# A mixture-of-experts block on one core: 58 feed-forward units of one form in engine loops, five token groups, roots and sigmoid from exp and ln

## What is computed

```python
def _mlp(x, wfc, wproj):
    h = jnp.square(jax.nn.relu(x @ wfc))
    return h @ wproj
shared = _mlp(x, w_fc_sh, w_proj_sh)
logits = xf @ router_w.T
scores = jax.nn.sigmoid(logits)
_, idx = jax.lax.top_k(scores + balance_bias, 2)
tw = jnp.take_along_axis(scores, idx, axis=-1)
tw = tw / (tw.sum(-1, keepdims=True) + 1e-20)
combine = (jax.nn.one_hot(idx, E) * tw[..., None]).sum(1)
h = jnp.square(jax.nn.relu(jnp.einsum('nc,ech->neh', xf, w1)))
y = jnp.einsum('neh,ehc->nec', h, w2)
routed = jnp.einsum('nec,ne->nc', y, combine)
...
h = h + _L0_attn_ref(_layernorm(h), ...)
h = h + _L0_ffn_ref(_layernorm(h), ...)      # shared + routed
```

## Time and profile before

| | us |
|---|---|
| median of three runs | 1073.99 (1067.09 to 1076.02) |
| the profiled execution | 1071.89 |
| its span | 1069.8 |
| PE busy | 633.5 |
| DVE busy | 723.8 |
| ACT busy | 480.2 |
| POOL busy | 301.6 |

### The profile page before, as it was taken

The page is one execution under the profiler, slowest core; times in us unless marked ns, Lnnn a source line. Parts: engine busy times, 40 slices in busy tenths (PEclk is TensorE's granted clock), DMA queues, the critical chain, the costliest instruction groups (busy, mean ns, idle before and its releaser), DMA issues.

```text
span 1069.8 us, 20111 instructions
## 1 busy us (share of the span) xinstructions
PE 633.5 (59%) x6510; PEld 480.5 (45%) x6510; DVE 723.8 (68%) x1727; ACT 480.2 (45%) x826; POOL 301.6 (28%) x269
## 2 busy tenths in 40 slices
PE   3669899045750777058888884412221389959462
PEld 2669699034640444025455553311111267747341
DVE  3314454378995999789999999888342575527265
ACT  3112253023445454058888885444311158747330
POOL 2111000056861111013232221103363700141455
PEclk9989799566695555556555555555555689969685
DMA  7953462220000222022222224410111324537343
GB/s 184 243 140 101 117 147 85 79 64 1 0 1 27 68 83 62 14 43 33 45 39 45 39 39 99 190 52 33 42 60 44 118 75 136 163 105 202 87 121 115
DMA packets 150683, 89.35 MB, mean 84 GB/s; under 512 B 88376, under 2 KB 143232, under 8 KB 150496
## 3 DMA queue, kind: packets, MB, share of 16 engines
q1 hardware_dynamic: 142768, 68.94, 25.3%
q0 software_dynamic: 7856, 19.68, 6.3%
HBM read 45.62 MB, written 28.51 MB: 69 GB/s over the span
## 4 chain that ended last, share of the span: by engine, by line
PE 24%; SPq 20%; DVE 19%; issue 15%; another core or an unknown queue 9%; ACT 6%; DMA 4%; POOL 4%; DVEq 0%; POOLq 0%; ACTq 0%
PE ps L1641 19%; SPq L564 7%; ACT R L718 3%; DMA R<-h_rows 2%; DVE M L1224 2%; DVE M L1225 2%; SPq L536 2%; SPq L543 2%; SPq L542 2%; SPq L544 1%; POOL R L711 1%; PE ps L1715 1%; PE ps L1896 1%; SPq L484 1%
## 5 line engine op out<-in xcount | busy, mean ns | idle before, releaser
L1641 PE MATMUL ps<-R 128*128 128x256 f16 (+6 forms) x2024 | 310.6, 308 | 91.9 <-issue 42.5
L1641 PEld LDWEIGHTS ps<-R 128*128 128x128 f16 (+3 forms) x2024 | 220.8, 131 | 154.7 <-issue 113.8
L718 ACT ACTIVATE R<-ps 128x768 f16<-128x768 f16 (+5 forms) x217 | 139.7, 662 | 183.9 <-remote 74.6
L1641 PE MATMUL ps<-M 32*128 32x68 bf16 (+4 forms) x1192 | 101.7, 245 | 99.3 <-DMA M<-R 65.9
L1641 PEld LDWEIGHTS ps<-M 32*128 32x128 bf16 (+3 forms) x1192 | 65.7, 116 | 151.3 <-issue 61.2
L721 ACT ACTIVATE R<-R,sc 128x512 f16<-128x512 f32 (+11 forms) x107 | 83.8, 839 | 92.8 <-POOL R L669 41.1
L711 POOL DMA_INDIRECT R<-y_by_tile,M x68 | 65.5, 963 | 143.7 <-DMA y_by_tile<-R 106.2
L683 POOL TENSOR_TENSOR R<-R,M 128x884 f32<-128x884 f32 x32 | 53.2, 1662 | 148.2 <-ACT M L840 148.2
L702 POOL DMA_INDIRECT x_by_expert<-R,M x68 | 66.1, 973 | 88.3 <-DVEq L1517 68.5
L718 ACT ACTIVATE R<-R 128x512 f16<-128x512 f32 (+4 forms) x101 | 64.7, 642 | 57.7 <-POOL R L652 20.4
L1641 PE MATMUL ps<-M,R 128*68 128x192 f16 (+2 forms) x430 | 47.1, 259 | 52.3 <-DVE R L1410 21.9
(11 more groups left out here) (281 smaller groups left out, 1148.4 us busy)
## 6 DMA issues: line engine op xcount, KB each, us to landing
R<-x_by_expert SPq DMA_DIRECT2D x41, 192.0 KB
y_by_tile<-R SPq DMA_DIRECT2D x41, 192.0 KB
R<-in_x_dram SPq DMA_DIRECT2D x12, 576.0 KB, 11.5
M<-R SPq DMA_DIRECT2D x16, 260.0 KB, 2.3
M<-R SPq DMA_DIRECT2D x32, 130.0 KB, 2.0
R<-w_split SPq DMA_DIRECT2D x1, 4032.0 KB, 23.2
R<-h_rows SPq DMA_DIRECT2D x4, 816.0 KB
R<-h_rows SPq DMA_DIRECT2D x1, 3264.0 KB, 14.3
```

The source lines that it names most:

```text
L718: return act.activation(out_, in_, ACT.Copy)
L1641: return pe.matmul(o, a, b, start=start, stop=stop, skip_group_check=True)
```

## The change

The feed-forward part and the groups are written anew.

- `WINDOWS` has five groups of 1, 4, 4, 4 and 4 pairs, and `SHARED_FIRST` is 12.
- All 58 units have one form. The rows of the shared pairs are stored to `x_by_expert` too, behind the routed ones (`SHARED_ROW`). SP loads the rows of every unit by a row number from a table, into one of eight sets (`XR`); TensorE turns them (`turn_unit`); ScalarE copies every result to `yr` and SP stores it in `y_by_unit`. For a pair's shared part SP loads its stored result again (`load_shared`) and VectorE adds it at the start of `combine`; `add_shared` is gone. `LAG` is 2.
- TensorE, ScalarE, VectorE and SP run the units in engine loops, two units a turn on TensorE, four on ScalarE, two or eight on VectorE, eight on SP. TensorE's groups are a loop as well. Since the set and the expert aren't known when the loop is written, TensorE reads three numbers of a table `rows_i` in each unit: the set's place before the transposes, the weights' place before `up` and again before `down`.
- `rows_i` lies on one partition: `make_table` now has 40 columns and 6 scan steps, and two of its columns go over TensorE and PSUM to that partition; `unit_rows` writes the shared units' part early.
- The roots are Exp(0.5 Ln v), and the sigmoid is Exp on ScalarE followed by an addition and a reciprocal on VectorE in `choose`. Normalising moves from VectorE to ScalarE (`x2_high`). The weights of all tokens are worked out once behind the table (`weigh`) and no longer in each `choose`.
- The combining starts at unit 33, one pair for two units, and pairs 12 to 16 are combined after the last unit. `combined` starts at 4, so that POOL may gather four pairs before the first is combined.

The core of the diff:

```diff
-WINDOWS = [(0, 5), (5, 12), (12, 17)]
-SHARED_FIRST = 10
+WINDOWS = [(0, 1), (1, 5), (5, 9), (9, 13), (13, 17)]
+SHARED_FIRST = 12
...
-            def load_tile(t):
-                wait(sp, "tile_turned", t - 3)
-                at = sp.value_load(table[t:t + 1, 1:2], min_val=0, max_val=XROWS - TILE)
+            for i in range(PAIRN):
+                sp.wait_ge(sem("rows2"), i + 1)
+                at = SHARED_ROW + TILE * i
+                sp.dma_start(xg[at:at + TILE, :].rearrange("(a p) c -> p a c", p=P), rows2[:, 2 * i:2 * i + 2, :]).then_inc(sem(f"x_rows{i // SHARED_FIRST}"), 16)
+            def load_unit(u, slot_, turn_):
+                wait(sp, "unit_turned", u - XR + 1)
+                wait(sp, f"xr{slot_ % 2}", 16 * (turn_ * (XR // 2) + slot_ // 2))
+                at = sp.value_load(rows_i[0:1, 1, bass.ds(u, 1)], min_val=0, max_val=XROWS - TILE)
...
+            def load_shared(i, slot_, turn_):
+                sp.wait_ge(sem("combined"), i + 1)
...
             def roots(k):
-                act.activation(rs2[:, 1, t], rs2[:, 0, t], ACT.Sqrt).then_inc(sem("ln2_sqrt"), 1)
+                chain(act, "scalar_step", act.activation(rs2[:, 1, t], rs2[:, 0, t], ACT.Ln))
+                act.activation(rs2[:, 1, t], rs2[:, 1, t], ACT.Exp, scale=0.5).then_inc(sem("ln2_sqrt"), 1)
             def x2_high(i):
-                act.wait_ge(sem("xf"), i + 1)
+                act.wait_ge(sem("ln2_done"), window_of(i) + 1)
+                for j in range(2):
+                    n = 2 * i + j
+                    last = ident_(xf[:, i % 2, j, :], hf[:, n, :], scale=rs2[:, 2, n:n + 1], bias=rs2[:, 0, n:n + 1])
...
             def choose(w):
+                ch(ts(s, s, 1.0, None, ALU.add))
+                ch(dve.reciprocal(s, s))
...
-            for w in range(3):
-                turn_window(w)
-                rank(w)
+            with pe.Fori(0, NW - 1) as w:
+                for j in range(4):
+                    turn_rows(w * 4 + 1 + j, j)
+                    if j >= 1:
+                        route(w * 4 + j, j - 1)
+                route(w * 4 + 4, 3)
+                rank(w + 1, w * 8 + 2, 8)
...
-            def turn_tile(t):
+            def turn_unit(u, par, half):
+                pe.wait_ge(sem(f"xr{par}"), half * 16 + 16)
+                wait(pe, "unit_x", u - 1)
+                at = pe.value_load(rows_i[0:1, 2, bass.ds(u, 1)], min_val=0, max_val=(XR - 1) * 4 * C)
+                        last = pe.transpose(o[:, (2 * k + j) * P:(2 * k + j + 1) * P], xr_flat[:, bass.ds(at + 2 * C * j + c, P)], ident_f[:, :])
...
-            def load_expert(u):
-                if kind == "r":
-                    expert_at.append(pe.value_load(table[i:i + 1, 0:1], min_val=0, max_val=E * WB))
+            def up(u, par, half):
+                at = pe.value_load(rows_i[0:1, 0, bass.ds(u, 1)], min_val=0, max_val=E * WB)
...
+            def down(u, par, half):
+                at = pe.value_load(rows_i[0:1, 0, bass.ds(u, 1)], min_val=0, max_val=E * WB)
...
-            for u in range(UNITS + LAG):
-                if 0 <= t + 1 < ROUTED:
-                    turn_tile(t + 1)
-                if u < UNITS:
-                    load_expert(u)
-                    up(u)
-                if u >= LAG:
-                    down(u - LAG)
+            pipeline(pe, [(turn_unit, 0), (up, 1), (down, 1 + LAG)], UNITS)
```

More of the change, by code:

```diff
@@ L64, with pipeline @@
 C0 = 0.35815147
-def pipeline(eng, stages, groups):
+def pipeline(eng, stages, groups, ring=2):
     last = max(lag for _, lag in stages)
-    lead = last + 2 + (groups - last) % 2
+    lead = last + 2
+    lead += (groups - lead) % ring
     def step(s):
@@ L413, in window_of @@
             return [i < b for _, b in WINDOWS].index(True)
[L415 to L428, removed]
+        COMBINE_FROM = 33
+        FOURS = 3
         block = ctx.enter_context(nc.Block())
@@ L904, in x2_window @@
-            def x2_window(w):
-                first, end = WINDOWS[w]
-                for i in range(first, end + 1):
-                    if i < end:
-                        x2_high(i)
-                    if i > first:
-                        x2_out(i - 1)
-            for i in range(8):
+                act.activation(scores[:, t, :], ps[:, 6, t.start * E:t.stop * E].rearrange("p (i e) -> p i e", e=E), ACT.Exp, scale=s1(W_RU)).then_inc(sem("sigmoid"), 1)
+            for i in range(3):
                 y_whole(i)
@@ L938, in high @@
-            def high(u):
-                act.wait_ge(sem("relu2"), u + 1)
-                wait(act, "h_used", u - 3)
-                copy(hh[:, u % 4], hs[:, u % 2]).then_inc(sem("high"), 1)
-            def relu(u):
+            x2_high(0)
+            y_whole(3)
+            x2_out(0)
+            exponentials(0)
+            y_whole(4)
+            roots(1)
+            for w in range(1, NW):
+                f, end = WINDOWS[w]
+                more = w < NW - 1
+                if more:
+                    y_whole(end)
+                x2_high(f)
+                if more:
+                    y_whole(end + 1)
+                x2_high(f + 1)
+                x2_out(f)
+                if more:
+                    y_whole(end + 2)
+                x2_high(f + 2)
+                x2_out(f + 1)
+                x2_high(f + 3)
+                x2_out(f + 2)
+                if more:
+                    y_whole(end + 3)
+                x2_out(f + 3)
+                exponentials(w)
+                if more:
+                    roots(w + 1)
@@ L1626, in _ @@
[L1626 to L1635 removed]
+                        h = hf[:, bass.ds(i * 2 + j, 1), :].rearrange("p o c -> p (o c)")
@@ new lines, in combine, with unit @@
+                        w = wt[:, bass.ds(i * 2 + j, 1), k:k + 1].rearrange("p o k -> p (o k)")
+                        last = dve.scalar_tensor_tensor(h, gb[:, slot_, j, k, :], w, h, ALU.mult, ALU.add)
+                    last.then_inc(sem("part_in" if k == 0 else "combined"), 1)
+            def unit(u, par):
+                if not (isinstance(u, int) and u == 0):
+                    low(u - 1, 1 - par)
+                relu2(u, par)
+            unit(0, 0)
+            unit(1, 1)
+            unit(2, 0)
@@ L1638, in _ @@
+            for i in range(4 * FOURS, PAIRN):
+                combine(i, i % 4, i // 4)
         @block.tensor
```

520 lines of the change are left out of this document (261 added, 259 removed).

## The result

The changed kernel takes 1213.34 us (median of four runs, 1209.32 to 1225.79) against 1073.51 for the kernel before: 1.133 times as long, 95% interval 1.127 to 1.139. Its profiled execution took 1213.61 us, with a span of 1211.7.
POOL's timeline after: the first scatter of each group, with the idle time ahead of it in brackets.

What follows compares the result with a forecast made beforehand. TensorE's sequencer was taken to pace the units, with results held during POOL's scatter bursts. Unit 0 at 864, 282 for units, 14 for gathers and pipeline end, 20 behind: 1180 span, plus 2: 1182 us; range 1115 to 1230.

Steps and rivals of the forecast that it cites:

- The unit of TensorE: Unit loop: loads and address computations on TensorE's sequencer make 5.13 us per unit against 2.54, 282 us over 55 steps.
- rival 2: Unit loop: load groups overlap part of their 0.65 us, 3.9 us a unit, total 1115 us; chance 0.11.
- That the branch costs 0.2 us and fetches nothing: TensorE's unit loop: the branch takes 0.21 us, and no turn fetches code, as in the attention's loops.
- Rival 3: Unit loop: register work runs ahead of the array, units stay at 2.54 us, total 1022 us; chance 0.07.
- The groups: Token groups: POOL's 20 us scatter run plus 13 us behind it for each held group; last slots at 846.
- The tail: VectorE between last slots and unit 0: tables 6.5, weights 2.6, y rows 8.9, together 18 us; unit 0 at 864.
- Rival 1: Token groups: runs of 16 scatters end before the hold builds up, unit 0 at 828, total 1146 us; chance 0.14.
- 8 us for held ones: Unit loop: gathers tied to the loop, four per two units; first window-sized runs still hold something, 8 us.
- Rival 4: Unit loop: gathers hold ScalarE there too, 12 pairs at 5 us more each, total over 1230 us; chance 0.05.
- the end: Behind the last unit: result, store, reload, shared part, last pair's gathers, adding and store, 20 us.
- At no cost: Units: more sets ahead and shared rows over DRAM change nothing; the wait they can remove is 0.7 us.
- Table loads: Roots and sigmoid: six table loads of 1.283 us go; the three before roots lie beside VectorE's work, giving nothing.

## Why the prediction was right, by its steps

The time, 1213.3, lies 31 above the 1182 and inside the range; the direction and the cause are those of the forecast. It lies outside 1150 to 1205, which the forecast gave for its own case: the wide range, and not the sum, covers the holds in the loop.

*The unit of TensorE*: forecast 5.13 us, measured 5.0 between VectorE's steps and 5.2 from branch to branch. Three edits moved the number of loads and addresses by one group up, one group and six addresses down, and to what it was before; units went to 5.85, 3.59 and 2.45. That is shown, not only read, and rival 2 with its 3.9 falls with it.

*That the branch costs 0.2 us and fetches nothing*: 208 ns at the median again over 26 turns, and three and one packets in the instruction queues in 865 to 1185. That is four packets for 26 turns, so there is none for each turn. In the loop of eight units there are six packets for six turns, and there it is the branch, 208 ns at the median and 233 at most, and the units' 3.59 us that speak against a fetch.

*Rival 3, register work that hides behind queued matmuls*, didn't come: the array did run behind the sequencer in the kernel before, but a pace is set by the slower of the two, and here that is the sequencer, with 5.0 us a unit against the array's 2.26 in the earlier trace rows.

*The groups*: forecast 33 us each and last slots at 846; measured 33.4 and 836.7, since the first came 9 us earlier. *The tail*: forecast 18, measured 18.3, and 5.2 of hold that the forecast had not. *Rival 1*, groups not held, didn't come on the chips that hold; on the third chip it did, with the last slots at 810.3 in the kernel with written-out units and paced gathers. Unit 0 at 864, measured 860.1.

*"8 us for held ones"* is the term that was mis-sized. The four gaps of 16.5, 17.2, 17.1 and 12.7 us are 43 above four units of 5. The forecast took the gathers to be tied to the loop, four for two units. But `combined` starts at 4, so POOL waits for a group's tiles and then sends twelve in a row. With gathers in runs of four the units took 34 us less. Rival 4, the loop is held as well, so came in part: it had 60 us for it, the forecast 8, and 43 were measured, nearer to the rival. This term, 35 too small, and the end, 22 instead of 20, less the 4 at unit 0 and a little for units of 5.0, make the 31 us.

*At no cost*, the forecast for the sets ahead and the shared rows over DRAM, holds for the first half of the units only. In the edit with written-out units they are all there, and from unit 0 to unit 32 it takes 84.0 us, where the kernel before takes 94.4 with its gap of 13.5. From there on it takes 122.4 against 109.1. Some 5 us of that are longer holds; the rest goes with VectorE, which there is busy for 20.0 of 24.7 us (968.0 to 992.7, between two holds) and now adds the stored shared part of every pair in these units (read from the trace, not tested). The forecast had this at nothing, and in the changed kernel's units of 5 us it is hidden. Table loads: nothing, as far as 0.4% tells. Five groups alone: the forecast charged them to the end, and in the kernel before they cost nothing there.

So of the 140 us, 110 are TensorE's unit loop, shown by taking it away. Of the other 30, the 20 ahead of unit 0 are read from the traces; how they would fall to groups, weighing and the trip over TensorE wasn't separated. Nor do they all reach the end: the kernel before waits 11 us in its third unit, beside its last scatters, and in the two edits that moved its first unit, by 9.4 us later and by 3.1 earlier, the end stayed.

## What to carry to other kernels

Before a unit of work goes into an engine loop, count what its sequencer must do for it: here 0.65 us for a number loaded from SBUF, 0.75 to 0.85 with its index, and 0.12 for each matmul whose address comes from a register. Against 26 matmuls of 2.3 us together that budget is soon gone, and no view of busy time shows it; the spacing of the sequencer's own instructions does. What can be known when the loop is written (a set, by unrolling as far as the ring is long) should be.

Long unbroken runs of indirect DMAs are worth breaking up, if only with useless work, where a trace shows late results beside them (35 us here); what it gains on the chip without a hold wasn't measured, since the changed kernel itself wasn't run there.

## What the runs showed of the hardware

On two of the three chips, runs of 12 and more indirect DMAs by POOL held TensorE's matmuls and their results: ScalarE's longest wait for an unknown releaser was 15.0 us in the kernel before and 14.5 in the changed one. What was slowed is TensorE's sequencer, and SP's: single instructions of 46 ns elsewhere took up to 715 and 706 ns. With pauses of 2.1 us behind every fourth scatter, ScalarE had no such wait from 700 us up to unit 0, and the first one, at 843.7 us, was 3.8 us. With gathers in runs of four, waits of 4.7 us at the longest were left in the units. Chips differed in it: on two the kernel before took 1073 us, on a third 996, and there no such wait appears in any of the four traces. Why is open; no run here looks into it, and none shows whether the hold stands when no trace is taken.

The loops' branch took 208 ns at the median on TensorE's sequencer (31 turns before, 26 after), and a number loaded from SBUF 0.30 to 0.31 us at the median, with 0.15 us of register work behind it.
